# GpSimd's two log-decay tiles of the delta-rule heads, issued right behind the state decay instead of behind the halos

## The reference

```python
g = jnp.exp(-jnp.exp(A_log) * jax.nn.softplus(a + dt_bias))
beta = jax.nn.sigmoid(b)
def step(Sstate, inputs):
    q_t, k_t, v_t, g_t, beta_t = inputs
    retrieved = jnp.einsum('bhkv,bhk->bhv', Sstate, k_t)
    error = v_t - g_t[..., None] * retrieved
    update = k_t[..., :, None] * (beta_t[..., None] * error)[..., None, :]
    Snew = g_t[..., None, None] * Sstate + update
    o_t = jnp.einsum('bhkv,bhk->bhv', Snew, q_t)
    return (Snew, o_t)
```

## Time and profile before

| | us |
|---|---|
| median of 3 runs | 4043.57 (4041.36 to 4048.10) |
| the profiled execution, its own time | 4039.44 |
| its span | 4037.6 |
| PE busy over the span | 3452.8 (86%) |
| DVE busy | 2312.6 (57%) |
| ACT busy | 1845.2 (46%) |
| POOL busy | 1580.2 (39%) |

### The profile page before, as it was taken

The page is one execution under the profiler, slowest core; times in us unless marked ns, Lnnn a source line. Parts: engine busy times, 40 slices in busy tenths (PEclk is TensorE's granted clock), DMA queues, the critical chain, the costliest instruction groups (busy, mean ns, idle before and its releaser), DMA issues. The chain is left out here.

```text
span 4037.6 us, 62353 instructions
## 1 busy us (share of the span) xinstructions
PE 3452.8 (86%) x19651; PEld 2714.7 (67%) x19682; DVE 2312.6 (57%) x4563; ACT 1845.2 (46%) x4568; POOL 1580.2 (39%) x2989
## 2 busy tenths in 40 slices
PE   3799999999999999999899388869979999973993
PEld 1688888888888888888777244448856666663441
DVE  2577767677776767777532577755536546532223
ACT  2556656555665656566421055534434435432110
POOL 2566666666666666666500100045532000003103
PEclk9899999999999999999989699989989999995996
DMA  2111112111111211111144400023353220116324
GB/s 67 47 50 46 43 47 53 48 51 50 46 43 47 53 48 49 52 45 43 52 148 128 168 11 13 11 68 106 104 169 140 73 83 12 72 41 224 128 89 154
DMA packets 422631, 294.64 MB, mean 73 GB/s; under 512 B 130352, under 2 KB 347312, under 8 KB 421328
## 3 DMA queue, kind: packets, MB, share of 16 engines
q1 hardware_dynamic: 415056, 272.07, 22.3%
q0 software_dynamic: 5120, 16.78, 1.3%
q10 hardware_dynamic: 2304, 4.20, 0.3%
HBM read 179.22 MB, written 113.77 MB: 73 GB/s over the span
## 5 line engine op out<-in xcount | busy, mean ns | idle before, releaser
L684 DVE SCALAR_TENSOR_TENSOR gd_conv<-gd_pre,gd_cur_a,gd_conv 128x512 f32<-128x512 f32 x384 | 457.3, 1191 | 46.2 <-ACT gd_conv L834 39.3
L511 PE MATMUL gd_PJ<-xn_lead,gd_w_rest 128*128 128x512 f32 x1024 | 452.0, 441 | 6.1 <-DVE gd_w_rest L677 6.1
L511 PE MATMUL gd_PJ<-xn_lead,gd_w_lead 128*128 128x512 f32 x1024 | 411.5, 402 | 0.0
L511 PE MATMUL gd_PJ<-xn_rest,gd_w_lead 128*128 128x512 f32 x1024 | 409.2, 400 | 0.0
L950 POOL TENSOR_TENSOR gd_T<-gd_T,gd_prod 32x14 f32<-32x14 f32 (+6 forms) x896 | 305.9, 341 | 70.2
L947 POOL TENSOR_TENSOR gd_prod<-gd_L,gd_T 32x14 f32<-32x14 f32 (+6 forms) x896 | 278.7, 311 | 70.7
L511 PEld LDWEIGHTS gd_PJ<-xn_lead,gd_w_lead 128*128 128x128 f32 x1024 | 197.8, 193 | 46.4
L511 PEld LDWEIGHTS gd_PJ<-xn_lead,gd_w_rest 128*128 128x128 f32 x1024 | 201.5, 197 | 36.4 <-DVE gd_w_rest L677 8.1
L2493 POOL MEMSET ms_rank<- 128x1 f32 x8 | 0.3, 98 | 561.3 <-POOLq L55 561.3
L511 PEld LDWEIGHTS gd_PJ<-xn_rest,gd_w_lead 128*128 128x128 f32 x1024 | 200.9, 196 | 27.5
L2203 PE MATMUL sa_B<-sa_kT,sa_qT 128*128 128x512 f32 (+3 forms) x512 | 182.2, 480 | 28.9 <-DMA sa_qT<-turned_queries_keys 17.0
(11 more groups left out here) (403 smaller groups left out, 9054.1 us busy)
## 6 DMA issues: line engine op xcount, KB each, us to landing
turned_queries_keys<-f_wq SPq DMA_DIRECT2D x16, 1280.0 KB, 6.0
triangles<-gd_Lo SPq DMA_DIRECT2D x64, 256.0 KB, 3.3
gd_W<-turned_image SPq DMA_DIRECT2D x64, 256.0 KB, 2.9
gd_T<-inverse_image SPq DMA_DIRECT2D x64, 256.0 KB, 3.3
gated_outputs<-gd_og SPq DMA_DIRECT2D x64, 256.0 KB, 2.6
go_ogt<-gated_outputs SPq DMA_DIRECT2D x16, 1024.0 KB, 6.8
sa_qT<-turned_queries_keys SPq DMA_DIRECT2D x16, 1024.0 KB, 5.6
gathered<-sa_blank SPq DMA_DIRECT2D x39, 256.0 KB, 4.5
```

What stands on the lines that cost most here:

```text
L511: mm = pe.matmul(bank, w_parts[wp][:, j, k, :], rhs, start=(k == 0 and wp == 1), stop=(k == KT - 1 and wp + xp == 0))
L684: nc.vector.scalar_tensor_tensor(out=conv[:, j], in0=pre[:, parm, j, :, d:d + P], scalar=cur[:, 4 * j + d:4 * j + d + 1], in1=conv[:, j], ...
```

## The change

In `slot` of GpSimd, the two log-decay tiles stand right behind the state decay `Sd` (in slot 0 right behind the solve) and ahead of the three halos. The wait for `darg` (PE has read the tiles of the slot before), which stood at the halo of v, moves to the front of the slot, ahead of the solve. No instruction is added or taken away.

```diff
                 if has1:
+                    if has3:
+                        pool.wait_ge(darg, n + 3)
                     start_solve(n + 1, back)
...
                     nc.gpsimd.tensor_tensor(Sd[:], S[:], bc(end[:, par, :], P), ALU.mult).then_inc(sd_ready, 1)
+                if has3:
+                    if has2 and not has1:
+                        pool.wait_ge(darg, n + 3)
+                    for part, col in zip(lgm, (P_LG, P_LGR)):
+                        at = col + c3 * B
+                        lg = ptab[:, bass.ds(h3, 1), at:at + B].rearrange("p o n -> p (o n)")
+                        tt = nc.gpsimd.tensor_tensor(part[:], bc(lg, P), later.unsqueeze(1).to_broadcast([P, B, P]), ALU.mult)
+                    tt.then_inc(lgm_ready, 1)
                 if has2:
                     pool.wait_ge(k_pre, n + 3)
                     halo(par, c2, PK, k_halo)
@@
                     pool.wait_ge(v_pre, n + 4)
-                    if has2:
-                        pool.wait_ge(darg, n + 3)
                     halo(parm, c1, PV, v_halo)
-                if has3:
-                    for part, col in zip(lgm, (P_LG, P_LGR)):
...
-                    tt.then_inc(lgm_ready, 1)
```

More of the change, by code:

```diff
@@ L984, in slot @@
                     pool.wait_ge(v_pre, n + 4)
-                    if has2:
-                        pool.wait_ge(darg, n + 3)
                     halo(parm, c1, PV, v_halo)
-                if has3:
-                    for part, col in zip(lgm, (P_LG, P_LGR)):
-                        at = col + c3 * B
-                        lg = ptab[:, bass.ds(h3, 1), at:at + B].rearrange("p o n -> p (o n)")
-                        tt = nc.gpsimd.tensor_tensor(part[:], bc(lg, P), later.unsqueeze(1).to_broadcast([P, B, P]), ALU.mult)
-                    tt.then_inc(lgm_ready, 1)
                 if has2:
```

## The result

The changed kernel takes 4119.76 us (median of four runs, 4117.09 to 4129.74), against 4045.76 (4041.36 to 4048.10) for the kernel before: ratio 1.0189 [1.0169, 1.0209], that is 74 us more. The forecast was 4104, +61. The profiled execution of the changed kernel took 4129.74 us, with a span of 4128.0 and a mean granted clock of 0.928; it is the longest of the four, so its trace shows about 10 us more than the median, and 90 more than the profiled execution of the kernel before.

A forecast was written before the change was run, and what follows sets the result against it. PE was taken to set the pace, busy 1,699 of 1,816 us, with 109.7 us idle in the wait for the second log-decay tile. Terms -7 + 33 + 25 + 10 = +61 on 4043.6 gave 4104; range 4035 to 4140 (8 in 10).

The forecast's parts named there:

- The darg wait costs nothing: Front of each GpSimd slot: PE raises darg well before GpSimd asks for it, so moving the wait costs 0 to 0.1 us a slot.
- Slot 0, -7 us: Slot 0 of 14 heads: tiles start where the halos did, 0.5 us earlier; PE still slow by its clock; -7 us.
- Slots 1 and 3, q taps passed over for 1.99 us more, +33: 15 heads each: a q tap also sits out both tiles, Pm comes later; 1.1 us a slot, +33 us.
- the first two q taps of slot 1 take some 5 us: Sign in DVE's timeline that the forecast is right; q taps of 1.5 us each at most would show it wrong.
- Slot 2, `once` and the whole sequence up to `Dm`, +25: 15 heads: DVE's `once` waits through tiles, halo of v and Dm; v taps and Pm come later; +1.65 us each, +25.
- The clock, +10: PE's new waits in slots 1 to 3 bring stretches at half clock; +10 us, bounds -35 to +50.
- the lower end, 4075: Lower end of the forecast's own span to 4125: Dm doesn't join in slot 2, -26, and no loss of clock.
- Turns with the tiles (4039): Rival: DVE's operations and GpSimd's tiles go in turns after all; -5 us together, 4039; chance 0.14.
- The wait goes and nothing comes in its place (3996): Rival: tiles fall into free time of DVE, PE's wait for them goes; 47 us faster, 3996; chance 0.15.
- The clock in most slots (4145): Rival: PE's clock falls in most slots; +51 from the slots and +50 of clock, 4145; chance 0.10.

## Why the prediction came out right

The mechanism was right: with no wait between them, the tiles join W16 and `Sd`, and DVE is kept out of all of it. Two waits of GpSimd, each on its own work, take the loss away (4015.89 and 4012.17 instead of 4119.76), and a narrow operation in front brings the same pattern about where it wasn't (4.33 us, 45 times), while a wide one doesn't. That the sequence starts with an operation on 32 partitions, which was read from a few rows, is borne out by that pair, with the reservation made there. What happens inside the engine, the idle part running ahead, was called a reading, and no run here observed it.

The number is closer than the working deserves, and part of that is luck. Forecast were -7 for slot 0, +58 of lateness in slots 1 to 3, and +10 of clock. The traces show -36 for slot 0 with its clock, +59 of idle time and +55 of clock in slots 1 to 3. Two terms were wrong, by 29 and 45 us, in opposite directions.

Step by step:

- *The darg wait costs nothing.* Right: within 0.25% at most, and no term of it in the trace.
- *Slot 0, -7 us.* Right in sign, far too small. The tiles start right behind W16, but the wait shrank by 1.3 us and not by 0.5; in the experiment with slot 0 alone by 0.5, and there the time fell by 14. The forecast read the clock from head 7, 5.6 us at 0.50 behind L647, and gave its loss back only as a bound (-3.3 a slot). In the mean of 14 heads the time at 0.50 near this wait was 5.1 us, and it fell to 2.4: to nothing in four heads, to half in five, and not at all in five. The table's -1.87 in the interval behind slot 0 holds this and slot 1's own 1.09.
- *Slots 1 and 3, q taps passed over for 1.99 us more, +33.* The price was right (4.96 for 2.96), the slots weren't: it happened in slots 2 and 3, so the sign "the first two q taps of slot 1 take some 5 us" failed. What was late next in slot 3 was missed: not `Pm`, 0.44 behind, but the bank that the squares hold, 1.25.
- *Slot 2, `once` and the whole sequence up to `Dm`, +25.* It happened in slot 1. There `once` and `twice` shared it, 3.55 and 1.70. PE waited 2.60 for `Pm`; 2.7 had been forecast. In slot 2 itself `once` alone took 5.5 us in heads 0 and 2 only.
- The exchange seems to have one cause, which the prediction missed: it moved single events in the timeline of before and held the phases of the engines fixed. GpSimd's solve of slot 1 now begins 19.3 us ahead of that slot's L647 instead of 22.0, and in slots 2 and 3 mostly 22 to 25 instead of 21 and 22; so W16 meets other work of DVE in each slot than before. The two heads in which `once` is passed over in slot 2 are the two in which that solve begins only 19.3 us ahead. No run tested this by itself. Since each pattern kept its price, the idle time of slots 1 to 3 came out as forecast.
- *The clock, +10.* Much too small. The stretches at 0.50 add up to 75 us before and 143 after in the heads, so half of 68, +34 net: +55 in slots 1 to 3 and -20 at slot 0. It is the term that was most mis-sized. The new waits were forecast at the right sizes, but the clock behind them was charged in slot 2 alone, and half of that was taken back.
- *The sum.* -7 + 33 + 25 + 10 = +61 against +74 by the medians and +79 in the heads of the two traces. With the clock's +34 in place of +10 it would have been +85; that slot 0 gave back 15 us of idle time and not 7 takes the 8 off again. And the lower end, 4075, doesn't follow from its own terms: 4104 less 26 less 10 is 4068.

**The rivals.** Turns with the tiles (4039): no, each tile took 1.03 us; yet this is what the wait behind the solve makes of it, at 4016. The wait goes and nothing comes in its place (3996): no, 112.7 us of other waits came. The clock in most slots (4145): for slots 1 to 3 this rival had it right. There are 37 stretches at half clock in 15 heads instead of 15, and those behind the new waits cost 55 us, where it had +50. What it lacked is the 36 us that slot 0 gave back.

**What stays open.** In slot 1 `once` got in behind lgm_rest, and `twice`, which asked at 1057.60 during the halo of k, was passed over by two halos and `Dm`. That part of the sequence has no narrow operation at its start, only one of 12 columns. Whether it is the short operation or the earlier W16 that carries on was not separated. Nor was the number of partitions separated from the number of elements on each.

## What to carry to other kernels

When work is moved earlier on an engine that shares something with another, look at what now stands directly behind what: the wait that was taken out may have been the gap through which the other engine got in. If that is so, the order need not be given up; a wait of the engine on its own last instruction can give the gap back, here for 0.07 to 0.19 us. And an instruction of 0.17 us that takes 3.55 names its cause by its end: find what ended on the other engine in the same 0.05 us. One head isn't all heads either: slot 0's clock, read from head 7 alone, looks cured, and in ten of 14 heads it isn't.

## What the runs showed of the hardware

- GpSimd operations that followed an operation on 32 partitions without an unmet wait kept a two-input operation of DVE out for up to six further instructions (three halos, `Dm` and two tiles behind W16): a tap of 0.74 us took 4.96 behind W16 there and 4.33 behind the added narrow operation, and three taps took 3.69 (in turns) behind a wide one.
- GpSimd's wait for its own last operation left it idle for 0.07 us (1005.38 to 1005.45) or 0.19 us, and that was enough to bring the turns back. The time saved in the changed kernel was 104 us.
- GpSimd's memset into the tiles took 0.52 us, and `twice` took its own 0.17 us beside it.
- The same wait of PE doesn't always bring the same clock. Around 3.50 us of idle in slot 0 of the kernel before, the granted clock was at 0.50 for 6.8 us in seven heads and for 3.4 in six. Behind 2.21 us in slot 0 of the changed kernel it was at 0.50 for 3.4 us in ten heads and not at all in four. Behind 2.60 us in slot 1 it was so for 3.4 us in ten heads, for 6.8 in three, and not at all in two.
